# Two of a decoder's attentions with eight heads packed per output product, and a third with one combined query-key weight

## What is computed

```python
# layer 0 self-attention: 16 heads of 16, causal
attn = softmax(q*scale @ k.T + causal_bias);  out = concat_heads(attn @ v) @ w_out.T + b_out
# layer 1 self-attention: one head of 256
q = x @ W_query;  k = x @ W_key;  v = x @ W_value
scores = einsum('bie,bje->bij', q, k) / sqrt(256)
attn = softmax(scores, axis=1);   out = einsum('bij,bie->bje', attn, v)
# layer 1 cross-attention: 16 heads of 16, keys and values from the context
out = concat_heads(softmax(q @ k.T) @ v) @ Wo + bo
```

## Time and profile before

| what | us |
|---|---|
| median of three runs (range) | 2405.68 (2405.28 to 2407.26) |
| the profiled execution's own time | 2410.23 |
| its span | 2408.4 |
| PE busy in the span | 2086.6, 87% |
| DVE, ACT, POOL busy | 1446.7, 1214.8, 767.5 |

### The profile page before, as it was taken

How to read it: one execution, slowest core, us unless ns; L and a number is a source line. 1 busy time by engine, 2 the same in 40 slices (tenths; PEclk the granted TensorE clock), 3 DMA queues, 4 the chain that set the end, 5 groups by cost and what they waited for, 6 DMA issues and landing times. The chain is left out here.

```text
span 2408.4 us, 33268 instructions
## 1 busy us (share of the span) xinstructions
PE 2086.6 (87%) x11559; PEld 1184.7 (49%) x11586; DVE 1446.7 (60%) x2698; ACT 1214.8 (50%) x2773; POOL 767.5 (32%) x1082
## 2 busy tenths in 40 slices
PE   6888899889998689999999986989899967788887
PEld 3333344344343445565555554556566643445445
DVE  4665566466773265666887975565744345557645
ACT  2455445544646265566887860757532324354342
POOL 4251220220010200121543541574642322443333
PEclk8899899999999899999999998989999988899898
DMA  6445333433421200000110104100001166544320
GB/s 153 111 74 138 79 64 87 85 76 65 73 56 38 65 21 5 28 27 9 62 51 34 51 34 181 40 7 27 9 29 48 49 123 115 127 92 93 75 67 34
DMA packets 132520, 156.60 MB, mean 65 GB/s; under 512 B 36493, under 2 KB 102929, under 8 KB 132258
## 3 DMA queue, kind: packets, MB, share of 16 engines
q1 hardware_dynamic: 132354, 154.47, 26.8%
HBM read 107.55 MB, written 46.86 MB: 64 GB/s over the span
## 5 line engine op out<-in xcount | busy, mean ns | idle before, releaser
L531 ACT ACTIVATE pbuf_sb<-psB 128x512 f32<-128x512 f32 (+1 forms) x608 | 330.1, 573 | 288.1 <-PE psB L409 238.5
L717 DVE TENSOR_REDUCE negm_sb<-psA 128x1 f32<-128x640 f32 (+6 forms) x352 | 352.3, 1027 | 187.9 <-PE psA L397 180.7
L1258 ACT ACTIVATE pw_sb<-psA,nmx_sb 128x154 f32<-128x154 f32 x512 | 191.9, 389 | 133.6 <-DVE nmx_sb L1403 133.6
L406 PE MATMUL psB<-qst_sb,kst_sb 99*128 99x512 bf16 (+3 forms) x768 | 238.8, 341 | 16.8 <-issue 5.1
L395 PE MATMUL psA<-kst_sb,qst_sb 96*128 96x512 bf16 (+3 forms) x768 | 202.9, 341 | 23.8 <-DVE negm_sb L717 22.7
L1403 DVE TENSOR_REDUCE nmx_sb<-psA 128x4 f32<-128x616 f32 x128 | 101.9, 796 | 125.1 <-PE psA L1027 124.9
L423 PE MATMUL psO<-pbuf_sb,V_sb 128*32 128x512 f32 (+3 forms) x1536 | 166.8, 515 | 11.0 <-ACT OT_sb L517 8.9
L406 PEld LDWEIGHTS psB<-qst_sb,kst_sb 99*128 99x128 bf16 x768 | 76.3, 100 | 182.2 <-ACT pbuf_sb L531 129.1
L2919 DVE TENSOR_REDUCE negm_sb<-psA 128x2 f32<-128x320 f32 x256 | 116.1, 481 | 72.0 <-PE psA L2682 67.5
L2802 ACT ACTIVATE pb_sb<-psB 128x512 f32<-128x512 f32 x160 | 92.8, 601 | 131.8 <-PE psB L2692 128.6
L2449 DVE TENSOR_REDUCE nma_sb<-psA 128x1 f32<-128x1024 f32 x32 | 39.1, 1222 | 142.4 <-PE psA L2046 142.4
(11 more groups left out here) (308 smaller groups left out, 4568.9 us busy)
## 6 DMA issues: line engine op xcount, KB each, us to landing
qst_sb<-parts_dram SPq DMA_DIRECT2D x192, 128.0 KB, 4.6
rden_sb<-dens_dram SPq DMA_DIRECT2D x128, 128.0 KB, 2.6
parts_dram<-parts_sb SPq DMA_DIRECT2D x32, 384.0 KB, 2.9
kst_sb<-parts_dram SPq DMA_DIRECT2D x96, 128.0 KB, 7.5
x_dram<-X_sb SPq DMA_DIRECT2D x64, 128.0 KB, 1.7
y_dram<-yw_sb SPq DMA_DIRECT2D x16, 512.0 KB, 2.8
Y_sb<-y_dram SPq DMA_DIRECT2D x16, 512.0 KB, 9.1
parts_dram<-partsb_sb SPq DMA_DIRECT2D x16, 384.0 KB, 3.0
```

Source lines behind the costliest of these rows:

```text
L406: last = nc.tensor.matmul(psB[:, k, at:at + hi - lo], kst[0:MAX_ROWS, gg % 3, h, i * P:(i + 1) * P], qst[0:MAX_ROWS, gg % 3, h, lo:hi], st ...
L531: nc.scalar.activation(pbuf[:, key % 2, heads[0]:heads[-1] + 1, lo:hi], psB[:, (nb.n - 1) % 2, 0:len(heads) * (hi - lo)] .rearrange("p (h ...
L717: nc.vector.tensor_reduce(out=negm[:, gg % 2, heads[0]:heads[-1] + 1, j], in_=psA[:, (na.n - 1) % 2, :].rearrange("p (h n) -> p h n", h=le ...
L1258: last = nc.scalar.activation(pw[:, m % 2, h, :], psA[:, m % 2, at:at + K], ACT.Exp, bias=nmx[:, m % 2, h:h + 1], accum_out=psx[:, m % 3, ...
```

## The change

**Packing (stages 1 and 4).** `OT` has two slots instead of six. A new buffer `OTC` of four slots holds eight heads in 128 partitions, 16 each, without gaps. After the denominator store of each group SP issues four DMAs that copy the 16 value rows of each head from `OT` to half a slot of `OTC`. `rden` has the same packed layout, so that each broadcast goes to 16 partitions. POOL scales one packed slot for each pair of groups, and a batch has two products per tile instead of four. The output weights are loaded by one DMA each in their plain order; the zeroing of `wo_a0` and `wo_x1` and the waits on it are gone. ACT's copy into `OT` now waits until the slot's last occupant has been copied and its denominators stored; SP's copies wait until the `OTC` slot was last projected.

**Stage 3.** The query projection and `qa` are gone. PE makes W_key W_query^T once (four products of 256 columns), ACT copies it, scaled by 1/16, to `wqk`, and the keys are projected with it; the scores are products of `ka` and the transposed input `XT3`, which has two buffers now. Both weights come transposed from the host.

```diff
             def reciprocals(gg):
                 sp.wait_ge(o_free, 2 * (gg + 1))
-                sp.dma_start(dens_dram[0], OT[HD:P:32, gg % OTN, :]).then_inc(dens_stored, 16)
+                sp.dma_start(dens_dram[0], OT[HD:P:32, gg % 2, :]).then_inc(dens_stored, 16)
+                if gg // 2 >= OCN:
+                    sp.wait_ge(var_ready, NT * ((gg // 2 - OCN) // KC + 1))
+                for h in range(4):
+                    at = 64 * (gg % 2) + HD * h
+                    sp.dma_start(OTC[at:at + HD, gg // 2 % OCN, :], OT[32 * h:32 * h + HD, gg % 2, :]).then_inc(ot_moved, 16)
...
-                if gg > 0:
-                    sp.wait_ge(ot_scaled, gg)
+                if gg > 1:
+                    sp.wait_ge(ot_scaled, gg // 2)
                 for h in range(4):
-                    sp.dma_start(rden[32 * h:32 * h + 32, :],
-                                 dens_dram[1, h:h + 1, :].broadcast_to([32, S])).then_inc(inv_loaded, 16)
+                    at = 64 * (gg % 2) + HD * h
+                    sp.dma_start(rden[at:at + HD, :],
+                                 dens_dram[1, h:h + 1, :].broadcast_to([HD, S])).then_inc(inv_loaded, 16)
...
             def project_out(b, j):
                 if j == 0:
-                    pe.wait_ge(wo_loaded, 16 * 5)
-                    pe.wait_ge(ot_scaled, G * (b + 1))
+                    pe.wait_ge(wo_loaded, 16 * 2)
+                    pe.wait_ge(ot_scaled, KC * (b + 1))
                 k = slot_a()
-                gemm(psA[:, k, 0:D], lambda g: OT[:, (G * b + g) % OTN, j * P:(j + 1) * P], lambda g: wo_a0[:, g, :],
-                     G).then_inc(a_full, 1)
+                gemm(psA[:, k, 0:D], lambda c: OTC[:, (KC * b + c) % OCN, j * P:(j + 1) * P], lambda c: wo_a0[:, c, :],
+                     KC).then_inc(a_full, 1)
...
             def copy_out(gg, c):
                 act.wait_ge(pv_done, 8 * gg + 4 * c + 4)
-                if gg >= OTN:
-                    act.wait_ge(var_ready, NT * ((gg - OTN) // G + 1))
-                nc.scalar.activation(OT[:, gg % OTN, c * 512:(c + 1) * 512], psO[:, c, :], ACT.Copy).then_inc(o_free, 1)
+                if gg >= 2:
+                    act.wait_ge(ot_moved, 64 * (gg - 1))
+                    act.wait_ge(dens_stored, 16 * (gg - 1))
+                nc.scalar.activation(OT[:, gg % 2, c * 512:(c + 1) * 512], psO[:, c, :], ACT.Copy).then_inc(o_free, 1)
...
-                if k >= 2 and early_groups(k - 2) is not None:
-                    scale_values(early_groups(k - 2))
+                done = early_groups(k - 2) if k >= 2 else None
+                if done is not None and done % 2 == 1:
+                    scale_values(done // 2)
...
                 for n in range(NC):
                     last = gemm(psA[:, 0, n * 512:(n + 1) * 512], lambda k: ka[:, k, j * P:(j + 1) * P],
-                                lambda k: qa[:, b % 2, k, n * 512:(n + 1) * 512], KC)
+                                lambda k: XT3[:, b % 2, k, n * 512:(n + 1) * 512], KC)
...
-            def project_qk(qk, e, c, n):
-                w = wk_a1 if qk == "k" else wq_a1
+            def combine_weights():
+                k = slot_c(("wqk",))
+                for c in range(KC):
+                    last = gemm(psO[:, k, c * D:(c + 1) * D], lambda i: wk_a1[:, i, c * P:(c + 1) * P], lambda i: wq_a1[:, i, :], KC)
+                last.then_inc(c_full, 1)
+
+            def project_k(e, c, n):
                 pe.wait_ge(t_act, T_FREED[("xt", e, 2 * n + 1)])
+                pe.wait_ge(c_act, C_FREED[("wqk",)])
...
-                    for qk in ("k", "q"):
-                        for c in range(KC):
-                            project_qk(qk, e, c, m - 6)
+                    for c in range(KC):
+                        project_k(e, c, m - 6)
...
-                    if j == 7 and 0 <= gg - 3 < GROUPS:
-                        scale_values(gg - 3)
+                    if j == 7 and 0 <= gg - 3 < GROUPS and (gg - 3) % 2 == 1:
+                        scale_values((gg - 3) // 2)
```

More of the change, by code:

```diff
@@ L480, in _ @@
             pe.wait_ge(a_free, na.n)
-            for g in range(G - 1):
-                pe.wait_ge(ot_scaled, G * (B - 1) + g + 1)
-                for j in range(NT):
-                    nc.tensor.matmul(late_tile(psA, j), OT[:, (G * (B - 1) + g) % OTN, j * P:(j + 1) * P], wo_a0[:, g, :],
-                                     start=(g == 0 and j < 4), stop=False, skip_group_check=True)
-            pe.wait_ge(ot_scaled, G * B)
+            pe.wait_ge(ot_scaled, KC * B - 1)
+            for j in range(NT):
+                nc.tensor.matmul(late_tile(psA, j), OTC[:, (KC * B - 2) % OCN, j * P:(j + 1) * P], wo_a0[:, 0, :],
+                                 start=(j < 4), stop=False, skip_group_check=True)
+            pe.wait_ge(ot_scaled, KC * B)
             for j in range(NT):
@@ L596, in _ @@
                         rest_of(u)
-            nc.gpsimd.memset(wo_a0[:, :, :], 0.0).then_inc(wo_zeroed, 1)
-            pool.wait_ge(wo_zeroed, 1)
             def quantise(step):
@@ L1550, in decoder_kernel @@
     XR = sb("XR", [P, 2, NT, D], F32, third_stage)
-    XT3 = sb("XT3", [P, KC, S], F32, third_stage)
+    XT3 = sb("XT3", [P, 2, KC, S], F32, third_stage)
+    wqk = sb("wqk", [P, KC, D], F32, third_stage)
     xq = sb("xq", [P, NT, D], BF16, f0_stage, "right")
@@ L1660, in decoder_kernel @@
                     number_t(("xt", e, i))
-            for qk in ("k", "q"):
-                for c in range(KC):
-                    number_c((qk, e, c, m - 6))
+            if m == 6 and e == 0:
+                number_c(("wqk",))
+            for c in range(KC):
+                number_c(("k", e, c, m - 6))
         if m == 7 and e is not None:
@@ L2260, in copy_xt, with copy_weights, copy_k @@
                 act.wait_ge(t_full, T_SLOT[key])
-                nc.scalar.activation(XT3[:, :, 2 * i * P:2 * (i + 1) * P].rearrange("p c (n q) -> p n c q", n=2),
+                nc.scalar.activation(XT3[:, e % 2, :, 2 * i * P:2 * (i + 1) * P].rearrange("p c (n q) -> p n c q", n=2),
                                      psB[:, t_bank(key), :].rearrange("p (n c q) -> p n c q", n=2, c=KC),
                                      ACT.Copy).then_inc(t_act, 1)
-            def copy_qk(qk, e, c, n):
-                key = (qk, e, c, n)
+            def copy_weights():
+                key = ("wqk",)
                 act.wait_ge(c_full, C_SLOT[key])
-                dst = ka[:, c, n * 512:(n + 1) * 512] if qk == "k" else qa[:, e % 2, c, n * 512:(n + 1) * 512]
-                nc.scalar.activation(dst, psO[:, c_bank(key), :], ACT.Copy,
-                                     scale=1.0 if qk == "k" else D ** -0.5).then_inc(c_act, 1)
+                nc.scalar.activation(wqk[:, :, :].rearrange("p c n -> p (c n)"), psO[:, c_bank(key), :], ACT.Copy,
+                                     scale=D ** -0.5).then_inc(c_act, 1)
+            def copy_k(e, c, n):
+                key = ("k", e, c, n)
+                act.wait_ge(c_full, C_SLOT[key])
+                nc.scalar.activation(ka[:, c, n * 512:(n + 1) * 512], psO[:, c_bank(key), :], ACT.Copy).then_inc(c_act, 1)
             def copy_v(e, j):
@@ L2297, in _ @@
                 if m in (6, 7) and e is not None:
+                    if m == 6 and e == 0:
+                        copy_weights()
                     if m == 6:
@@ L2300, in _ @@
                             copy_xt(e, i)
-                    for qk in ("k", "q"):
-                        for c in range(KC):
-                            copy_qk(qk, e, c, m - 6)
+                    for c in range(KC):
+                        copy_k(e, c, m - 6)
                 if m == 7 and e is not None:
@@ L2602, in reciprocals @@
                 sp.wait_ge(o_free, 2 * (gi + 1))
-                sp.dma_start(dens_dram[0], OT1[HD:P:32, gi % OTN, :]).then_inc(dens_stored, 16)
+                sp.dma_start(dens_dram[0], OT1[HD:P:32, gi % 2, :]).then_inc(dens_stored, 16)
+                if gi // 2 >= OCN:
+                    sp.wait_ge(zc_full, ZC_SLOT[("o", (gi // 2 - OCN) // KC, NT - 1)])
+                for h in range(4):
+                    at = 64 * (gi % 2) + HD * h
+                    sp.dma_start(OTC1[at:at + HD, gi // 2 % OCN, :], OT1[32 * h:32 * h + HD, gi % 2, :]).then_inc(ot_moved, 16)
                 sp.wait_ge(dens_stored, 16 * (gi + 1))
```

89 lines of the change are left out of this document (44 added, 45 removed).

## The result

| | us |
|---|---|
| predicted | 2342 (2322 to 2370) |
| the changed kernel, median of 4 runs | 2339.9 (2333.5 to 2346.2) |
| the kernel before, median of 4 runs beside them | 2405.7 (2405.3 to 2407.3) |
| ratio | 0.9724 (95%: 0.9703 to 0.9745) |
| profiled execution, span | 2343.2 (before 2408.4) |

The account below looks back on a forecast made before the run. PE, busy 87% of the span, was taken as the bound, with waits deciding as much in stage 4. Terms -18 + 0.5 - 26 - 13.5 - 4.4 - 4 + 1.6 = -63.8 from 2405.7 gave 2342 us (2322 to 2370, 8 in 10).

Parts of the forecast that it names:

- Tiles of stage 1: Stage 1's 24 output tiles inside steps: half the products go, 0.75 us a tile (0.5 to 0.9), -18 (-12 to -22).
- End of stage 1: Last denominators' chain of stage 1: removed products worth nothing, load issued 0.4 us later, PE perhaps cold; +0.5 (-1 to +3).
- Stage 3: Query products go, 27.5 us; combining adds 1.8 at most or 0 in a wait; -26 (-22 to -28).
- Stage 4, POOL: Eight of sixteen scalings go: 2.7 us at the second batch's third group, 1.3 for all others; -4 (0 to -11).
- Stage 4, tiles and chains: Stage 4's thinner output tiles, -13.5 for three batches and -4.4 for the last, and four longer denominator chains, +1.6.
- DVE's plain step: Stage 4 tiles without attended values: 2.27 us between residuals, already as short as DVE allows, so they give nothing by themselves.
- PE arrives earlier at these places ... nothing more is won: Stage 4's four first-output-tile waits: the chain starts with ACT's copy and keeps its length, so PE's earlier arrival wins nothing.
- Chains: Stage 4, once a batch: four more issues cost 0.4 us where the store is quick; +0.4 each, +1.6 (-4 to +11.6).
- The sign that PE's wait at the first output tile should grow by what PE saved: At stage 4's four chains, PE's wait should be longer by about what PE saved ahead of it.
- the first (all of it, 2321): Rival, whole kernel: everything PE loses is won, -85, 2321 us; chance 0.15 for 2315 to 2330.
- The second (2368): Rival: DVE and the chains hold on, POOL's relief gives nothing, each chain 2 us more; -38, 2368 us; chance 0.16.
- The clock: Rival: thinner stage 1 steps let the clock fall once per tile, 1.8 us each, 43 less gain, 2385 us; chance 0.03.

Follow-up runs that it names:

- the parts alone: Three runs, each the kernel before with only the change's stage 3, stage 1 or stage 4 part: 2374.9, 2381.9 and 2382.2 us.
- POOL alone: Kernel before with stage 4's scaling for each batch's first and third groups cut to one column of 1024, output not the reference's: 2395.9 us, ratio 0.9974.
- the late copies: Changed kernel with each group's four copies issued behind the denominators' load instead of ahead of it, in both stages: 2338.8 us, 0.9732 of the kernel before.

## Why the prediction was right, and where its steps were not

The time came within 2 us of the forecast, which is better than the steps deserve: several were off by 3 to 4 us and cancelled. The last few us of the agreement are luck.

- **Tiles of stage 1**, forecast -18: -21 in both traces of the changed kernel, 0.87 a tile; less what the same stretch moved in untouched kernels, 17 to 21. Inside a batch it is 5.5 us for seven steps, 0.79 each, so the 0.75 holds. Its reason doesn't: in the first batch the seven steps give 0.34, 1.39, 0.86, 0.49, 1.09, 1.01 and 0.33 us, outside the 0.5 to 0.9 in five of seven, and the widest tile is not the smallest among them (8.68 to 7.59). The step that went wrong is the one that bounds a tile by DVE's idle time before its residual: the waits before the maxima shrink too.
- **End of stage 1**, forecast +0.5: +0.4 by the parts alone, at the same clock. The load was to be issued 0.4 us later and came 1.2 later, because a copy's issue costs 0.6 us and not the 0.43 of a broadcast; the shorter broadcasts (3.62 us from issue to DVE instead of 4.07) gave back 0.45. I took the issue's price from another kind of DMA.
- **Stage 3**, forecast -26: -30.3, outside the -22 to -28 given. The 27.5 us for the products held; mis-sized was the combining. I had it between +1.8 and 0, "may warm or not". It lies in a wait, costs nothing, and the next product behind it is warm; stage 3 gave 2.8 us beyond its removed products where I had allowed 1.5 the other way. The run with it moved back shows 4.3 us for its place alone. The rest is in part the clock again: the second batch's first key product, at 4.83 us before, took 3.60 in the recorded trace and 3.88 in two others.
- **Stage 4, POOL**, forecast -4: 5.0 in the stretch with the one shown place (3.4 with stage 4 alone changed, 3.3 with POOL alone), and 6.3 (2.6 to 10) for POOL alone in the time. Right in mechanism, and the 4 lies within the interval.
- **Stage 4, tiles and chains**, forecast -13.5, -4.4 and +1.6, together -16.3: the table's tiles give 3.6 + 2.2 + 5.2 + 4.0 = 15.0, and 4 us go at the stage's start, of which 2 to 3 also go where stage 4 is unchanged. Two errors lie under the good sum. DVE's plain step wasn't floored at 2.27 us but went to 2.12. And the sentence "PE arrives earlier at these places ... nothing more is won" looked at PE's waits only, and took the chain to keep its length. Behind a batch's output tiles it grew by 1.2 us while DVE became 1.0 us faster, so DVE's wait at its reciprocal, in the middle of its queue, went from 1.33 to 3.50 us. The move of that one instruction gives 4.7 us back in that stretch.
- **Chains**: store to load grew by 1.2 us (1.84 to 3.05) and not by 0.4, but store to scaling at the last batch was 11.87 us and is 11.65; DVE and POOL, busy with the bias until then, end it and not SP. A longer link in a chain costs nothing when another engine's queue holds the next one, which the late copies show; where DVE stands waiting for it, it costs what it is longer. The sign that PE's wait at the first output tile should grow by what PE saved did not come: 4.93 us where 4.88 stood, and 8.42 where 8.63 stood. The Trainium skill, "DMA: Bandwidth & Descriptors", section "Anatomy of one DMA — SWDGE (gpsimd) path", had given 0.6 us for the copies' bytes, an estimate from its 436 GB/s, and that for DMAs that GpSimd issues, where these are SP's. Here eight copies of half the size cost SP twice the issuing time and the chain 1.7 us with no byte more, so the count of DMAs set that part of the price. What the load behind them took longer, 0.8 us at one place and 0.4 at the end of stage 1 (2.00 us from its issue to the reciprocal, before 1.65), no run divides between bytes and count.

Of the rivals, the first (all of it, 2321) asked for 22, 27.5 and 27.5, and 8 for POOL; stage 3 gave more, stage 1 17 to 21, and stage 4 with POOL about 20 of its 35.5. The second (2368) had 12 and 24 for stages 1 and 3, which both gave more, and nothing for POOL. The clock did not fall in the thinner steps: the stretch from 200 to 400 us has 0.96, before 0.95.

```profile
200.00:400.00 200.00, 175.10 (x1207) 80.40 (x1205) 119.90 (x167) 102.01 (x188) 34.47 (x42) 0.96 0.44 92
```

## What to carry to other kernels

When one engine's work is cut, go through the queues of the other engines for instructions that wait for a DMA chain: the chain gets no shorter (here it got longer by 1.2 us), and whoever reached them late before now reaches them early, with everything queued behind. Small independent work is best put exactly into a known wait ahead of long products, where it costs nothing and keeps the clock up. And a link added to a chain has to be priced up to the next engine that joins it, not at the queue that issues it.

## What I had not expected of the hardware

A copy of 16 partitions by 4 KB inside SBUF took SP 0.60 us to issue (2.41 us for four, 4.96 for eight of half the size, so for SP's time the bytes don't matter), a broadcast of one row to 16 or 32 partitions 0.43 (1.71 us for four in both kernels). And the same program of stage 1 in two executions came to the same instruction at 304.35 us and 4.4 us earlier, with granted clocks of 0.91 and 0.93: a profile's place in the program isn't good to better than this, so single stretches are to be compared over several profiles, or between profiles with the same granted clock there.
